# Packed keys: two heads per tile, pair products on array halves, one maximum per pair

## The chip, the cores and the metric

The program runs on one core of one Trainium2 chip. The metric is the device time in microseconds of one execution; the median of three runs is compared. The engines are TensorE (matrix products into PSUM), VectorE, ScalarE, GpSimd (POOL) and SyncE, which issues most of the DMAs. PSUM has eight banks of 512 fp32 columns.

## What is computed

Four layers run over a batch of 4 sequences of 1024 tokens with 256 channels. What matters here is attention, in layers 0, 1 and 3:

```python
s = jnp.einsum('bhqd,bhkd->bhqk', q, k) * scale      # 16 score maps per batch, 16 channels each
s = jnp.where(mask, s, jnp.float32(-jnp.inf))         # causal
p = jax.nn.softmax(s, axis=-1)
out = jnp.einsum('bhqk,bhkd->bhqd', p, v)
```

Layer 0 and layer 3 have 16 heads; layer 1 has 8 differential heads, which are 16 score maps in pairs with a value of 32 channels per pair. Layer 0 goes on with a mixture of experts (2 shared, 16 routed, top 2), layer 1 with a gated FFN, layer 2 has a recurrent mixer and a ternary FFN, layer 3 eight LoRA experts on a gated FFN, top 2.

## The kernel before

Each layer is a loop over the four batches, and each batch a sequence of stages with a barrier between them. A stage is a block in which every engine has its own instruction list, ordered by hand, and engines wait for one another's semaphores. The three layers with attention share four pieces.

`attention_operands` normalises the input, projects q, k and v tile by tile (L354, eight tiles of 128 tokens), rotates q and k on VectorE (L407 to L412), splits each value into an fp16 high part and an fp16 rest (ScalarE L451, L454; POOL L484, L486) and stacks them so that one product over 128 rows gives the full-precision score. A q tile holds two heads of 64 rows each. A k tile holds one head: its 64 rows, and zeros in the other 64, so that k tile times q tile gives one head's score. TensorE turns 8 q and 16 k tiles per token tile (L340, L342) into banks 4 and 5 to 6; VectorE stores q (L369) and ScalarE stores k (L430).

`MaximumPass` finds each query's largest score, so that the exponentials can be shifted. It runs inside the expert stages: TensorE puts a block of scores (L552, up to 512 columns) and, on a diagonal block, a mask product (L555) into a bank, and VectorE reduces the bank to its maximum (L586). 192 blocks and 4 small turns (L545) are dealt out over the slots between the products of the experts by `share_out`. A bank is filled again when VectorE has read it. In layer 0's experts (`experts`: L1154 up, L1139 down, VectorE's sum L1187) the banks are 4 to 7 in turn; in layer 3 (`lora_experts`: L1657, L1660 first products, L1668 second, L1678 lower, L1695 and L1699 down) they are 6 and 7, and bank 6 also serves the low-rank products L1645 and `down`. The low-rank product of the second half of the tokens stands in the middle of the stage. The negated maxima go by DMA (L602) into two rows of each q tile, next to two rows of ones in k.

`attention` works on key tiles: TensorE makes transposed scores of one head (L628) with a mask product on the diagonal block (L631) into one of three pairs of banks (2 to 7), ScalarE takes the exponential (L673), and TensorE multiplies by the values (L647), 17 or 33 output rows for each head side by side in the array, into banks 0 and 1. With maps = 4 (layers 0 and 3) a step is four heads of one key tile: three scores, the values of the step before, the fourth score. With maps = 2 (layer 1) it is two heads: both scores, then the values of two steps before. The width W of a score is 1024 - 128 x (key tile), so a group of eight steps goes from 1024 to 128 columns; there are four groups, or eight in layer 1. L664 stores the sums of a group.

`attention_finish` turns the sums back and divides (L727, L765, L774).

Of the kernel before, what the change touches and what calls it, by code (L numbers as in the profile page):

```python
# [17 lines left out]
P = 128  # L18
# [9 lines left out]
NEG = -1.0e30  # L28
E_SH, E_RT, F0 = 2, 16, 128
# [7 lines left out]
ARENA = 43600  # L37
# [75 lines left out]
def setup_constants(nc, m, io):  # L113

    with stage(nc, "cleared", "selected", "psum_cleared", "tables_in", pool=True) as (block, cleared, selected, psum_cleared, tables_in):
        @block.gpsimd
        def _(pool):
            pool.memset(m.ident[:, :], 0.0).then_inc(cleared, 1)
            pool.memset(m.mask_qk[:, :], 0.0).then_inc(cleared, 1)
            pool.memset(m.mask_kq[:, :], 0.0).then_inc(cleared, 1)  # L120
# [10 lines left out]
            pool.affine_select(out=m.mask_kq[:, :], in_=m.mask_kq[:, :], compare_op=ALU.is_ge, fill=NEG,  # L131
# [165 lines left out]
def attention_operands(nc, m, a, src, batch, out_bias, wqkv, bias, table, rms, heads, vd):  # L297
# [19 lines left out]
    names = ["proj", "taken", "steps", "pool_done", "rotated", "hi", "lo", "stacked", "turned", "stored", "cleared",  # L317
             "rms_in", "rms_std", "squared"]
    with stage(nc, *names, *Normalisation.SEMAPHORES, pool=True) as (block, proj, taken, steps, pool_done, rotated, hi, lo, stacked, turned, stored,
# [3 lines left out]
        def kcols(buf, parity, slot, n=1, step=1):  # L323

            c0 = P * parity + 64 * parity + HD * slot
            v = a.ks[:, buf, :].rearrange("p (n c) -> p n c", c=2 * P)
            if n == 1:
                return v[:, :, c0:c0 + HD]
            return v[:, :, c0:c0 + HD * step * n].rearrange("p n (s c) -> p n s c", c=HD * step)[:, :, :, 0:HD]

        @block.tensor
        def _(pe):
            def turn(t):
                pe.wait_ge(stacked, 3 * (t + 1))
                if t >= 1:
                    pe.wait_ge(stored, 2 * t)
                psq = m.ps[:, 4, :].bitcast(F16)
                psk = m.ps[:, 5:7, :].rearrange("p a b -> p (a b)").bitcast(F16)
                for n in range(NM // 2):
                    pe.transpose(psq[:, n * P:(n + 1) * P], a.qs[:, t % 2, n * P:(n + 1) * P], m.ident_h[:, :])  # L340
                for n in range(NM):
                    last = pe.transpose(psk[:, n * P:(n + 1) * P], a.ks[:, t % 2, n * P:(n + 1) * P], m.ident_h[:, :])  # L342
                last.then_inc(turned, 1)
# [1825 lines left out]
```

## Time and profile before

| | us |
|---|---|
| median of three runs | 5175.5 |
| lowest, highest | 5164.4, 5177.24 |
| span of the profiled execution | 5169.3 |

The span is counted from the first to the last instruction. In a row of the profile `out<-in` names the tensors written and read, the numbers before it are partitions x elements, `x` counts instructions, and a bracket says how long the engine was idle before it and for whose result. An fp32 product shows as two instructions. `PEld` is the load of a product's stationary operand. The end of a product is modelled and lies after the time at which the next may start, so the throughput of TensorE is read from starts.

### The profile page before, as it was taken

Reading aid. Unit: us, or ns where it says so; the run is one execution under the profiler, and the core shown is the slowest. Engines: PE = TensorE matmul, PEld = TensorE weight load, DVE = VectorE, ACT = ScalarE, POOL = GpSimd, SP = SyncE. Lnnn points to the kernel's source line nnn. Section 1 sums busy time; section 2 is a strip of 40 time slices with the busy share of each in tenths; the row PEclk is TensorE's granted clock in tenths of the full one; section 3 lists DMA queues with packets and bytes.
Section 4 is the critical chain, followed back from the end, with each engine's and each line's share of the span. In section 5 each row is a group of like instructions: output and inputs, shape, how many; then the busy total and the mean of one; then the engine's idle time right before and its main releaser. Section 6 shows DMA issues by size and latency. Waiting matters only on the chain. (4 is left out here: it accounts for less than half of the span.)

```text
span 5169.3 us, 62879 instructions
## 1 busy us (share of the span) xinstructions
PE 4168.2 (81%) x22944; PEld 2388.1 (46%) x22944; DVE 2510.8 (49%) x5496; ACT 1934.0 (37%) x3242; POOL 557.6 (11%) x629
## 2 busy tenths in 40 slices
PE   6979979979828979798974786776887898888898
PEld 4635536446313644536352654655344443443443
DVE  5917738459162342415036446446643552651661
ACT  3163261441626355463622323323126116206206
POOL 1001010010011010100000201203211110210220
PEclk9999999989958989899986888888999899999999
DMA  2000000000030000000010000001000000000000
GB/s 81 1 2 1 1 1 1 1 1 1 2 110 1 1 1 1 1 1 1 1 47 0 1 0 0 0 0 43 1 1 9 1 1 10 1 1 10 1 1 9
DMA packets 44814, 45.06 MB, mean 9 GB/s; under 512 B 10320, under 2 KB 40784, under 8 KB 44496
## 3 DMA queue, kind: packets, MB, share of 16 engines
q1 hardware_dynamic: 37424, 31.89, 2.1%
q10 hardware_dynamic: 7072, 9.05, 0.6%
q8 instruction: 184, 3.01, 0.2%
q14 instruction: 134, 1.10, 0.1%
HBM read 36.22 MB, written 4.19 MB: 8 GB/s over the span
## 5 line engine op out<-in xcount | busy, mean ns | idle before, releaser
L586 DVE TENSOR_REDUCE arena<-ps 128x1 f32<-128x512 f32 (+3 forms) x1536 | 779.5, 550 | 219.6 <-PE ps L555 127.7
L673 ACT ACTIVATE arena<-ps 128x1024 f32<-128x1024 f32 (+7 forms) x1024 | 594.1, 660 | 119.5 <-PE ps L631 62.2
L628 PE MATMUL ps<-arena 128*128 128x512 f16 (+3 forms) x1536 | 392.4, 333 | 94.6 <-ACT arena L673 71.0
L552 PE MATMUL ps<-arena 128*128 128x512 f16 (+3 forms) x1536 | 414.6, 328 | 14.2 <-DVE arena L586 12.1
L765 DVE RECIPROCAL small<-ps 128x16 f32<-128x16 f32 x64 | 16.1, 251 | 782.7 <-PE ps L727 782.1
L673 ACT ACTIVATE attention<-ps 128x512 f32<-128x512 f32 (+7 forms) x512 | 302.5, 656 | 116.9 <-PE ps L631 78.1
L631 PE MATMUL ps<-mask_kq,ident_b 128*128 128x128 bf16 x1536 | 323.9, 221 | 0.0
L628 PEld LDWEIGHTS ps<-arena 128*128 128x128 f16 x1536 | 138.5, 98 | 399.3 <-ACT arena L673 336.2
L1732 ACT ACTIVATE arena<-ps 128x512 f32<-128x512 f32 x96 | 53.0, 595 | 681.7 <-PE ps L1668 578.0
L1170 ACT ACTIVATE arena<-ps 128x512 f32<-128x512 f32 x144 | 86.0, 597 | 592.1 <-PE ps L1154 592.0
L1154 PE MATMUL ps<-arena 128*128 128x512 f32 x576 | 302.6, 613 | 0.0
L647 PE MATMUL ps<-arena 128*17 128x512 f32 (+3 forms) x3072 | 297.4, 489 | 2.9 <-ACT arena L673 2.9
L647 PE MATMUL ps<-attention 128*33 128x512 f32 (+3 forms) x1536 | 296.0, 494 | 0.0
L552 PEld LDWEIGHTS ps<-arena 128*128 128x128 f16 x1536 | 144.7, 97 | 314.3 <-DVE arena L586 197.1
L1139 PE MATMUL ps<-arena 128*128 128x256 f32 x1152 | 289.0, 387 | 0.8 <-DVE arena L1187 0.8
L354 PE MATMUL ps<-arena 128*128 128x512 f32 (+1 forms) x768 | 275.3, 508 | 0.0
L782 DVE RECIPROCAL small<-ps 128x16 f32<-128x16 f32 x32 | 8.1, 254 | 496.2 <-PE ps L727 494.9
L1657 PE MATMUL ps<-arena 128*128 128x512 f32 x384 | 207.7, 623 | 27.6 <-DVE arena L1750 18.2
L1139 PEld LDWEIGHTS ps<-arena 128*128 128x128 f32 x1152 | 206.6, 190 | 38.2 <-issue 8.0
L1187 DVE SCALAR_TENSOR_TENSOR arena<-ps,arena 128x256 f32<-128x256 f32 x512 | 217.9, 474 | 10.0 <-PE ps L1139 9.0
L555 PE MATMUL ps<-mask_qk,ident_b 128*128 128x128 bf16 x1024 | 221.2, 220 | 0.0
L628 PE MATMUL ps<-attention 128*128 128x512 f16 (+3 forms) x768 | 202.2, 340 | 15.0 <-PEq L56 14.9
(271 smaller groups left out, 6995.9 us busy)
## 6 DMA issues: line engine op xcount, KB each, us to landing
making<-basis SPq DMA_DIRECT2D x16, 768.0 KB, 4.5
out<-x_all SPq DMA_DIRECT2D x8, 512.0 KB, 3.0
arena<-w_down SPq DMA_DIRECT2D x1, 2304.0 KB, 24.8
x_all<-x SPq DMA_DIRECT2D x2, 1024.0 KB, 13.8
x_all<-x ACTq DMA_DIRECT2D x2, 1024.0 KB, 19.7
arena<-arena SPq DMA_DIRECT2D x128, 4.0 KB
making<-w_gate_up SPq DMA_DIRECT2D x1, 2048.0 KB, 15.2
arena<-w_qkv SPq DMA_DIRECT2D x2, 768.0 KB, 6.2
```

What stands on the lines that cost most here:

```text
L354: last = pe.matmul(m.ps[:, 2 * (t % 2) + j, 0:w], m.xn_t[:, k, t * P:(t + 1) * P], wqkv[:, k, c0:c0 + w], start=(k == 0), stop=(k == KD - 1))
L552: last = pe.matmul(out[:, 0:w], a.q[:, hh // 2, qt * P:(qt + 1) * P], a.k[:, hh, c * CH:c * CH + w], start=True, stop=not diag)
L555: last = pe.matmul(out[:, w - P:w], m.ident_b[:, :], m.mask_qk[:, :], start=False, stop=True)
L586: dve.reduce_max(a.mp[:, h, qt, c:c + 1], out[:, 0:w], AX.X).then_inc(self.block_out, 1)
L628: last = pe.matmul(m.ps[:, bank + c, q0 - c * CH:CH], a.k[:, h, kt * P:(kt + 1) * P], a.q[:, h // 2, q0:(c + 1) * CH], start=True, stop=no ...
L631: last = pe.matmul(m.ps[:, bank + c, q0 - c * CH:q0 - c * CH + P], m.ident_b[:, :], m.mask_kq[:, :], start=False, stop=True)
L647: last = pe.matmul(m.ps[width * hh:width * hh + w, c, q0 - c * CH:CH], a.v[:, kt, vh, :], p, start=(kt == 0), stop=(kt == TC * (c + 1) - 1))
L673: act.activation(a.p[:, u % ring, kt * P:S], m.ps[:, bank:bank + 2, :].rearrange("p a b -> p (a b)")[:, kt * P:S], ACT.Exp, scale=HD ** -0 ...
L1139: last = pe.matmul(product(n, j), f.mid[:, n % 3, j * P:(j + 1) * P], wdown[:, e, :], start=True, stop=True)
L1154: last = pe.matmul(m.ps[:, n % 2, :], wup[:, e, k, :], m.xn_t[:, k, c * CH:(c + 1) * CH], start=(k == 0), stop=(k == KD - 1))
L1187: dve.scalar_tensor_tensor(m.acc[:, t, :], out, f.gate_w[:, t, e - E_SH:e - E_SH + 1], m.acc[:, t, :], ALU.mult, ALU.add).then_inc(added, 1)
L1657: pe.matmul(m.ps[:, 2 * (n % 2) + j, :], wt[:, k, i * P:(i + 1) * P], m.xn_t[:, k, c * CH:(c + 1) * CH], start=(k == 0), stop=False)
```

## The change

Keys are packed as queries are: a k tile holds two heads of 64 rows. A score product names the 64 rows of its head, so the two heads of a pair work on the two halves of the array and into different banks. The parts:

- `attention_operands`: 16 transposes per token tile instead of 24, into two alternating pairs of banks; one ScalarE instruction stores q and k; VectorE's store is gone; ScalarE and POOL write k in one instruction each instead of two.
- `MaximumPass`: an item is a block of two heads: two mask products first (on a diagonal block), then the two halves' products, then one maximum over 2 x w values. 96 items and 4 turns. In `experts` the items take the bank pairs 4, 5 and 6, 7 in turn; in `lora_experts` they all take 6, 7.
- `attention`: no mask product; a step scores its pairs, then does values. For key tiles 4 to 7 the two heads of a pair share one pair of banks and one exponential. VectorE cuts what lies above the diagonal by a minimum with a triangle of 3e38 and 0, in place, and values wait for that.
- `lora_experts`: both low-rank products at the start, in banks 4, 5 and 2, 3; `down` in banks 4, 5 and 0, 1; the order around the middle is other.

```diff
             def turn(t):
-                pe.wait_ge(stacked, 3 * (t + 1))
-                if t >= 1:
-                    pe.wait_ge(stored, 2 * t)
...
+                pe.wait_ge(stacked, 2 * (t + 1))
+                if t >= 2:
+                    pe.wait_ge(stored, t - 1)
...
-            def store(t):
-
-                dve.wait_ge(turned, t + 1)
-                dve.tensor_copy(a.q[:, :, t * P:(t + 1) * P],
-                                m.ps[:, 4, :].bitcast(F16).rearrange("p (n c) -> p n c", c=P)).then_inc(stored, 1)
...
+                act.activation(a.qk_t[:, :, :, t * P:(t + 1) * P].rearrange("p n j c -> p j n c"),
+                               m.ps[:, b0:b0 + 2, :].bitcast(F16).rearrange("p j (n c) -> p j n c", c=P),
+                               ACT.Copy).then_inc(stored, 1)
...
-        last = pe.matmul(out[:, 0:w], a.q[:, hh // 2, qt * P:(qt + 1) * P], a.k[:, hh, c * CH:c * CH + w],
-                         start=True, stop=not diag)
+        pair = g * self.maps // 2 + j
         if diag:
-            last = pe.matmul(out[:, w - P:w], m.ident_b[:, :], m.mask_qk[:, :], start=False, stop=True)
-        last.then_inc(self.block_in, 1)
+            for odd in range(2):
+                pe.matmul(out[:, odd, w - P:w], m.ident_b[:, :], m.mask_qk[:, :], start=True, stop=False,
+                          skip_group_check=True)
+        for odd in range(2):
+            half = slice(64 * odd, 64 * odd + 64)
+            last = pe.matmul(out[:, odd, 0:w], a.q[half, pair, qt * P:(qt + 1) * P],
+                             a.k[half, pair, c * CH:c * CH + w], start=not diag, stop=True, skip_group_check=True)
+        last.then_inc(self.pair_in, 1)
...
-        dve.reduce_max(a.mp[:, h, qt, c:c + 1], out[:, 0:w], AX.X).then_inc(self.block_out, 1)
+        dve.reduce_max(a.mp[:, 2 * j:2 * j + 2, qt, c], out[:, :, 0:w], AX.X).then_inc(self.pair_out, 1)
...
+                s = first_slot[v]
+                end = first_slot[v + 1]
+                if end > 3:
+                    pe.wait_ge(exped, end - 3)
...
+                    for odd in range(2):
+                        half = slice(64 * odd, 64 * odd + 64)
+                        b = bank(s + odd) + c if kt < TC else bank(s) + odd
+                        last = pe.matmul(m.ps[:, b, q0 - c * CH:CH], a.k[half, pair, kt * P:(kt + 1) * P],
+                                         a.q[half, pair, q0:(c + 1) * CH], start=True, stop=True)
...
-                pe.wait_ge(exped, maps * (n + 1))
+                pe.wait_ge(masked, pairs * (n + 1))
...
-                for hh in range(maps):
-                    score(maps * n + hh)
-                    if hh == maps // 2 and n >= lag:
-                        values(n - lag)
+                for j in range(pairs):
+                    score(pairs * n + j)
+                if n >= lag:
+                    values(n - lag)
...
+                dve.wait_ge(exped, first_slot[v + 1])
+                diag = a.p[:, 2 * v % ring:2 * v % ring + 2, kt * P:(kt + 1) * P]
+                dve.tensor_tensor(diag, diag, keep, ALU.min).then_inc(masked, 1)
...
-        mp.share_out([((n, i), up if i < KD else (per_step - KD * up) / TC, (4, 5, 6, 7))
+        mp.share_out([((n, i), up if i < KD else (per_step - KD * up) / TC, (4, 6))
...
-        fixed = {"down": 1, "second": 1.5, "lower": 0}
+        fixed = {"down": 0.5, "second": 0.5}
...
-        mp.share_out([(key, fixed.get(key[0], rate), (7,) if key[0] == "down" else (6, 7)) for key in slots])
+        mp.share_out([(key, fixed.get(key[0], rate), (6,)) for key in slots])
...
             pe.wait_ge(*weights)
             low(0)
+            low(1)
```

## Rows read from the trace of the kernel before

**Rows 1.** The page's first part: busy time of each engine.
```profile
PE 4168.2 (81%) x22944; PEld 2388.1 (46%) x22944; DVE 2510.8 (49%) x5496; ACT 1934.0 (37%) x3242; POOL 557.6 (11%) x629
```

**Rows 2.** Stretches: length, then busy PE, PEld, DVE, ACT, POOL, clock, DMA.
```profile
91.90:266.50 174.60, 171.12 (x786) 106.66 (x785) 159.97 (x399) 24.37 (x39) 0.00 (x0) 0.99 0.00 1
268.40:362.60 94.20, 83.25 (x704) 30.15 (x704) 0.00 (x0) 78.65 (x137) 0.00 (x0) 1.00 0.00 1
378.60:432.50 53.90, 37.13 (x272) 25.92 (x272) 40.49 (x82) 32.20 (x43) 15.46 (x24) 0.90 0.01 2
1601.30:1719.70 118.40, 117.66 (x704) 39.32 (x704) 0.00 (x0) 83.83 (x145) 0.00 (x0) 0.99 0.00 1
3637.00:3838.80 201.80, 184.54 (x712) 88.97 (x712) 131.18 (x252) 13.24 (x24) 45.65 (x36) 0.99 0.00 1
```

**Rows 3.** Timeline of layer 0's operands: start, length, engine, line.
```profile
46.25 0.68 DVE L381 TENSOR_TENSOR arena<-ps,arena 128x512 f32<-128x512 f32 x1
...
49.99 0.68 DVE L381 TENSOR_TENSOR arena<-ps,arena 128x512 f32<-128x512 f32 x1
...
62.59 0.68 DVE L369 COPY arena<-ps 128x1024 f16<-128x1024 f16 x1
...
63.19 0.68 DVE L381 TENSOR_TENSOR arena<-ps,arena 128x512 f32<-128x512 f32 x1
...
64.96 1.88 ACT L430 ACTIVATE arena<-ps 128x2048 f16<-128x2048 f16 x1 [1.01 <-PE ps L342]
...
67.03 0.68 DVE L369 COPY arena<-ps 128x1024 f16<-128x1024 f16 x1
```

**Rows 4.** Timeline of the same stage, the last turn.
```profile
80.27 0.61 PE L340 MATMUL ps<-ident_h,arena 128*128 128x128 f16 x8 [2.06 <-ACT arena L430]
```

**Rows 5.** Timeline of TensorE in layer 0's attention.
```profile
292.07 0.38 PE L628 MATMUL ps<-arena 128*128 128x512 f16 x1
...
292.29 0.22 PE L631 MATMUL ps<-mask_kq,ident_b 128*128 128x128 bf16 x1
...
293.32 0.38 PE L628 MATMUL ps<-arena 128*128 128x512 f16 x1
...
293.63 0.41 PE L647 MATMUL ps<-arena 128*17 128x128 f32 x8
...
297.12 1.91 PE L647 MATMUL ps<-arena 128*17 128x512 f32 x16
...
298.97 0.34 PE L628 MATMUL ps<-arena 128*128 128x384 f16 x1
```

**Rows 6.** Groups of L586 by form, whole span: busy, mean ns, idle before.
```profile
L586 DVE TENSOR_REDUCE arena<-ps 128x1 f32<-128x512 f32 x768 | 513.2, 684 | 132.9 <-PE ps L552 83.2 <-PE ps L555 44.3
...
L586 DVE TENSOR_REDUCE arena<-ps 128x1 f32<-128x128 f32 x256 | 72.1, 282 | 13.1 <-PE ps L555 11.4
```

**Rows 7.** Layer 0's attention: timeline, and the group of the widest exponentials.
```profile
292.76 3.77 ACT L673 ACTIVATE arena<-ps 128x1024 f32<-128x1024 f32 x4 [0.21 <-PE ps L628]
...
293.97 0.39 PE L628 MATMUL ps<-arena 128*128 128x512 f16 x1
...
303.29 2.60 ACT L673 ACTIVATE arena<-ps 128x768 f32<-128x768 f32 x4 [0.65 <-PE ps L628]
...
315.74 3.77 ACT L673 ACTIVATE arena<-ps 128x1024 f32<-128x1024 f32 x4 [0.21 <-PE ps L628]
...
L673 ACT ACTIVATE arena<-ps 128x1024 f32<-128x1024 f32 x16 | 15.1, 1028 | 0.6 <-PE ps L628 0.6
```

**Rows 8.** Line L774: an operation of VectorE over 256 values, min/median/max ns.
```profile
L774 DVE TENSOR_TENSOR x_all<-arena x32: 424/425/426, 365.0 to 1418.1; 128x256 f32 x32
```

**Rows 9.** Timeline of TensorE in the LoRA stage: idle time at the seam and in `down`.
```profile
3715.63 1.98 PE L1645 MATMUL ps<-arena 128*128 128x512 f32 x4 [1.57 <-DVE arena L1748]
...
3719.93 1.10 PE L1657 MATMUL ps<-arena 128*128 128x512 f32 x2 [2.32 <-DVE arena L1750]
...
3820.73 1.10 PE L1695 MATMUL ps<-arena 128*128 128x256 f32 x4 [2.15 <-issue]
```

More of the change, by code:

```diff
@@ L316, in attention_operands, with slots @@
         cos, sin = ([v.rearrange("p (h c) -> p h c", c=HD)] * NT for v in table)
-    names = ["proj", "taken", "steps", "pool_done", "rotated", "hi", "lo", "stacked", "turned", "stored", "cleared",
+    names = ["proj", "taken", "steps", "pool_done", "rotated", "hi", "stacked", "turned", "stored", "cleared",
              "rms_in", "rms_std", "squared"]
-    with stage(nc, *names, *Normalisation.SEMAPHORES, pool=True) as (block, proj, taken, steps, pool_done, rotated, hi, lo, stacked, turned, stored,
+    with stage(nc, *names, *Normalisation.SEMAPHORES, pool=True) as (block, proj, taken, steps, pool_done, rotated, hi, stacked, turned, stored,
                                cleared, rms_in, rms_std, squared, *norm_sems):
         norm = Normalisation(m, src, a.xn, m.xn_t, norm_sems, xload=batch, bias=out_bias)
[L323 to L329, printed above, removed]
+        def slots(stack, buf):
+            return stack[:, buf, :].rearrange("p (h s c) -> p h s c", h=NM, c=HD)
         @block.tensor
@@ L506, in __init__ @@
             i = 0
-            for h in range(self.maps):
+            for j in range(self.maps // 2):
                 for qt in range(NT):
                     for c in range(qt // TC + 1):
-                        self.items.append(("block", g, h, qt, c))
+                        self.items.append(("pair", g, j, qt, c))
                         i += 1
@@ L527, in share_out, with pair_banks @@
         assert len(self.banks) == len(self.items)
-    def bank(self, n):
-        return self.m.ps[:, self.banks[n], :]
+    def pair_banks(self, n):
+        return self.m.ps[:, self.banks[n]:self.banks[n] + 2, :]
     def tensor_item(self, pe, n):
         m, a = self.m, self.a
-        out = self.bank(n)
+        out = self.pair_banks(n)
         if self.items[n][0] == "turn":
@@ L608, in attention @@
 def attention(nc, m, a, maps, width):
-    groups = NM // maps
-    n_exp = NM * NT
+    groups, pairs = NM // maps, maps // 2
+    n_pair = pairs * groups * NT
     ring = a.p.shape[1]
     lag = 1 if maps == 4 else 2
-    with stage(nc, "scored", "exped", "summed", "evac") as (block, scored, exped, summed, evac):
+    first_slot, slots = [], []
+    for v in range(n_pair):
+        first_slot.append(len(slots))
+        if v // pairs % NT < TC:
+            slots += [(v, 0), (v, 1)]
+        else:
+            slots += [(v, None)]
@@ L616, in _, with place, bank, score @@
+    first_slot.append(len(slots))
+    def place(v):
+        n, j = divmod(v, pairs)
+        g, kt = divmod(n, NT)
+        return g, kt, g * pairs + j
+    def bank(s):
+        return 2 + 2 * (s % 3)
+    with stage(nc, "scored", "exped", "masked", "summed", "evac") as (block, scored, exped, masked, summed, evac):
         @block.tensor
         def _(pe):
-            def score(u):
-                n, hh = divmod(u, maps)
-                g, kt = divmod(n, NT)
-                h = g * maps + hh
-                if u >= 3:
-                    pe.wait_ge(exped, u - 2)
-                bank = 2 + 2 * (u % 3)
+            def score(v):
+                g, kt, pair = place(v)
+                s = first_slot[v]
+                end = first_slot[v + 1]
+                if end > 3:
+                    pe.wait_ge(exped, end - 3)
@@ L681, in _ @@
             store(groups - 1, 1)
+        @block.vector
+        def _(dve):
+            keep = m.tri[:, :].unsqueeze(1).broadcast_to([P, 2, P])
+            for v in range(n_pair):
+                g, kt, pair = place(v)
+                dve.wait_ge(exped, first_slot[v + 1])
+                diag = a.p[:, 2 * v % ring:2 * v % ring + 2, kt * P:(kt + 1) * P]
+                dve.tensor_tensor(diag, diag, keep, ALU.min).then_inc(masked, 1)
 def attention_finish(nc, m, a, maps, width, wout, out_scale, batch=None, stored=None):
```

222 lines of the change are left out of this document (97 added, 125 removed).

## Prediction, made before the changed kernel was run

> **What bounds the kernel now.** I read the page's first part, then one stretch per stage, then the instructions inside each. TensorE is busy 81% of the 5169.3 us span [rows 1], an average over unlike stages. One batch of each, in [rows 2]: the experts stage has TensorE at 171.1 of 174.6 us, VectorE at 160.0 beside it, so TensorE bounds it. Layer 0's attention has TensorE 83.3 and ScalarE 78.7 of 94.2: neither alone, but the chain between them. Layer 1's attention has TensorE 117.7 of 118.4. Layer 0's operands (53.9) have nothing full over the stage; inside it VectorE runs without gaps. The LoRA stage has TensorE 184.5 of 201.8, and 131.2 of VectorE. Each occurs four times, except that layer 3's attention and operands are like layer 0's: eight of those.
>
> **Operands (saves).** VectorE starts a period at 62.59 with the q store L369 and the next at 67.03: 4.43 us without a gap, of which L369 takes 0.60 (62.59 to 63.19). A period without it, 46.25 to 49.99, is 3.74 [rows 3]. The store goes to ScalarE, which already spends 1.88 on 2048 values of k; q and k together are again 2048. ScalarE's copies go from 0.63 + 2 x 0.40 to about 2 x 0.63, the POOL differences from three to two of the same size, the transposes from 24 to 16 per tile. None reaches 3.7 us a period (ScalarE 1.88 + 1.26; TensorE 2.6 of projections + 0.9). Five stores lie ahead of the last rotation: 5 x 0.6 = 3.0. At the end the last turn waited 2.06 for ScalarE's previous store [rows 4]; with two PSUM pairs it waits for POOL alone, 1.9 less. Together about 5.0 a stage (bounds 3 and 6.5), layer 1 the same: 12 x 5.0 = -60 us.
>
> **What a pair costs TensorE.** A full-array fp16 product of 512 columns holds it 0.215 us (292.07 to the mask at 292.29), or 0.42 ns a column, so a mask of 128 takes 0.055. The product at 293.32 has streamed by 293.53, but the narrow values product starts at 293.63. The 16 narrow ones from 297.12 go in four groups of four, 0.435 a group, so they have streamed by 298.87; the full product starts at 298.97. A change of array form costs 0.10 each way [rows 5]. No row shows the array split by rows. Split by columns the four products of a group run at once: 16 of 0.43 us take 1.91 and not 7 [rows 5]. I take row halves as equally concurrent, the nearest row (bound above: one after the other, as full products go), and the switch as 0.095 each way (bounds 0 and 0.19, two loads of 0.10 behind each drain).
>
> The Trainium skill, TensorEngine Tiling (Array Packing), Key Properties, says a change of tiling mode drains TensorE, without a price; by it alone splitting costs something wherever other forms stand between, and the row above prices it.
>
> **Experts (about nothing).** 192 blocks hold 16 heads x 4608 causal columns = 30.7 us of products; concurrent pairs save half, 15.4. Masks stay 128. Laying the 100 items on the slots by the code gives 91 runs of pair products between full-array work: 91 x 0.19 = 17.3. VectorE's maximum falls a little: 512 columns take 0.684, 128 take 0.282 [rows 6], so 1.05 ns a column plus 0.15; two joined save a start-up of 0.07 to 0.15, 96 times, hidden beside TensorE. But it now frees a pair only after 1.22 us and there are two pair buffers; I add 2 us. Sum +4 a stage (bounds -12 and +20), 4 x = +16.
>
> **Attention of layers 0 and 3 (saves).** Four exponentials of 1024 take 3.77, one 1.03: 0.91 apart (0.904 by the starts), which is W/1.2 + 51 ns; of 768, 0.69. But before the fourth of each step ScalarE sits idle, 0.65 at 768 [rows 7]; per group of eight steps the starts at 292.76 and 315.74 are 22.98 apart against 17.95 of work. The cause: the fourth score stands behind the values product. At W = 768 the chain is release 0.31 (an exponential lasts 0.12 beyond its slot, 1.03 against 0.904, and the product after it starts 0.19 later), score 0.32 + 0.06, switch, values of 896 at 1.67 ns = 1.49, switch, score up to its last product 0.16, and 0.38 to completion: 2.9, against three exponentials 2.07; stall 0.8, measured 0.65 to 0.8. The new order (both pairs, then values) gives: exponential 0.69, release 0.31, pair 0.32, switch 0.1, values 1.49, switch 0.1, next pair to its last product 0.05, completion 0.42, less 0.1 by which this sum exceeded the trace above: 3.38 a step against 2.76 of ScalarE work. In the same way W = 896 gives 3.8 and 640 3.0; W = 1024, behind short values, has ScalarE alone, 4 x 0.904 and a store of 512 columns at the same rate, 0.48: 4.15. The four joined steps need 6.6: ScalarE 5.2, plus the wait that the change adds. Values now wait for VectorE's minimum (256 values: 0.42 [rows 8] and two hand-overs, about 0.55), behind which TensorE's next scores queue; at the widths 256 and 128 two slots of exponentials (0.96, 0.53) don't cover it. Group 21.0, four 84, start-up 2.3: 86.5 against 94.2, -7.5 (bounds -14, ScalarE alone, and -3), 8 x = -60 us. The 128 masks leave, and ScalarE has 32 start-ups of 51 ns fewer; both are inside this sum.
>
> **Layer 1's attention (saves).** Per step TensorE does W/2.4 x 2 + 0.11 + 0.19 of scores, masks, switches and W/600 of values two steps back. Taking the larger of that and ScalarE's step, a group is 1.81 + 1.60 + 2.65 + 2.33 + 2.0 + 1.69 + 1.36 + 1.05 + a store 0.48 = 15.0; eight give 120 for 118.4, so the reading holds. With concurrent pairs and no masks: 1.81 + 1.60 + 2.2 + 1.95 + 1.68 + 1.42 + 1.15 + 0.88 + 0.48, plus 0.25 since a pair waits for the first half of the one before: 13.4, eight 107: -11.5 (bounds -18, -4), 4 x = -46 us.
>
> **LoRA stage (costs).** Before, the maxima had banks 6 and 7: TensorE filled one while VectorE read the other. Now all items use the one pair 6, 7, and each of the six slots of a unit has 1.15 items and only one fp32 product (0.86) between. From one item to the next for 512 columns: two masks 0.11, switch 0.095, product to completion 0.38, hand-over 0.04, maximum of 1024 values 1.22 (from 0.684 and 0.282 [rows 6]), hand-over 0.06: 1.90. TensorE's own work in that time: 0.11 + 0.19 + 0.21 + 0.86 = 1.37. Stall 0.53; at 384 columns 0.26, at 256 and 128 none; over the mix of twelve (6, 2, 2, 2) 0.31. An item directly behind another stalls 1.1. Per unit five of the first and one of the second, 2.6; 12 units 31 us. Behind TensorE's wait queue the next FFN products, and VectorE's gates behind those. Switches 92 x 0.19 = 17.5 against 15.4 saved. In return the second low-rank block moves from the middle to the front, where six VectorE operations (4.3) hold up the first items, TensorE some 3.5. The waits of the seam go: by starts 1.1, 1.7, 2.5 and 1.0, the second and third shown as 1.57 and 2.32 of idle; of `down` 1.1 twice, 1.2 and 2.3 (2.15 shown), two others of 1.6 and 0.9 [rows 9]: 14.5 in all. Waits of the old items, 3.9, go. Sum 31 + 2 + 3.5 - 14.5 - 3.9 + 2 for late gates = +20 (bounds 0 and +32), 4 x = +80 us.
>
> **Sum.** -60 + 16 - 60 - 46 + 80 = -70. Against the profiled 5169.3: 5099; the median of the runs is 6.2 above it, so 5105.
>
> **Rivals.** A: the halves run one behind the other. Place: every pair. Price: 15.4 in each of eight maximum passes = 123; in attention the pair lies on the chain, 7.6 x 8 = 61 and 6.1 x 4 = 24; together +208, 5313. It decides once the second product starts a third of the first's streaming (about 72 ns of 215) behind it. For: no row shows a row split. Against: the column split [rows 5]. Halfway, if each run of pairs loads its two weights behind the drain (0.095 more, 183 runs x 4): +70, 5175. The Trainium skill, TensorE: Matmul & The Clock Gate, Measured speedup vs the span model, has four row tiles at 3.07 times. By an estimate from that figure a pair would take 0.65 of serial, not 0.5, and the time would be 5167; it belongs to the halfway case.
>
> B: the single pair buffer of the LoRA stage costs nothing, since the stage has slack elsewhere: -80, 5025. For: 17 of its 201.8 us are idle time of TensorE now [rows 2]. Against: TensorE is in order, and each item must wait for a read of 1.22. C: the change leaves ScalarE and TensorE of attention coupled as before, another order but the same stalls; then -60 and -46 shrink to -20 and -25: 5166. For: the minimum adds a link; against: the fourth score no longer stands behind values.
>
> **How the numbers follow.** Forecast 0.66 (own range 5060 to 5150), A in full 0.12, halfway 0.08, B 0.07, C 0.07. Predicted 5105. Range 5030 to 5195: it leaves out A and the far half of B. A measurement of this kernel tells 0.3%, 15.5 us, from no change: below 5160 are nearly all of the forecast (0.64), B and a little of halfway and C, 0.74; within, parts of both, 0.09; above, A and the rest, 0.17.
>
> **What would show it.** Row-half products starting within 20 ns of each other; a gap of about 0.1 around each run; operands near 49, layer 1's 5 shorter too; layer 0's attention near 87, layer 1's near 107; experts within 5 of 174.6; LoRA near 222, with TensorE waiting for L586's successor. I am wrong if the second half starts late (experts above 190), or if the LoRA stage is not longer.

## The result and the profile after

The changed kernel takes 5199.8 us (median of four runs, 5198.2 to 5202.95) against 5175.3 for the kernel before (four runs too, 5164.4 to 5177.2). The ratio is 1.0053, with a 95% interval from 1.0039 to 1.0067. So it is slower, by a little more than the 0.3% that can be told from no change. The prediction was 5105, with 5030 to 5195 as its range: the sign was wrong, and the time lies outside the range.

The profiled execution of the changed kernel has a span of 5197.9 us, 28.6 more than before. Its first part answers to [rows 1]:

```profile
PE 3998.3 (77%) x20640; PEld 2097.8 (40%) x20640; DVE 2748.2 (53%) x5400; ACT 1889.1 (36%) x2762; POOL 511.6 (10%) x521
```

Every engine but VectorE does less: TensorE 170 us less, ScalarE 45 less. The time went up all the same. These are the stretches that answer to [rows 2]: experts, layer 0's attention, the LoRA stage, layer 1's attention and layer 0's operands. The columns are the length, busy PE, PEld, DVE, ACT and POOL, the granted clock of TensorE, and DMA.

```profile
88.10:269.20 181.10, 176.30 (x784) 97.62 (x783) 156.89 (x303) 24.38 (x39) 0.00 (x0) 0.99 0.00 1
271.00:365.00 94.00, 66.61 (x574) 13.95 (x572) 26.87 (x64) 75.33 (x105) 0.00 (x0) 0.85 0.00 1
3586.00:3817.00 231.00, 201.61 (x720) 83.49 (x718) 128.97 (x162) 13.87 (x25) 45.12 (x36) 0.97 0.00 1
1610.80:1720.10 109.30, 96.08 (x576) 23.14 (x572) 27.21 (x64) 81.49 (x113) 0.00 (x0) 0.96 0.00 1
378.30:430.80 52.50, 35.11 (x208) 23.57 (x208) 36.01 (x74) 30.77 (x35) 14.23 (x20) 0.79 0.01 2
```

The second row is the one to stop at. The stage has 17 us less of TensorE and 3 less of ScalarE than in [rows 2], and it is as long as before (94.3 us for 94.1 by first and last instruction; the other seven take 94.1 to 97.4). The number that changed for the worse is the granted clock, 0.85 instead of 1.00. The sums over the whole program, each stage counted from its start to the start of the next, are as follows. The products of the router, the first 7 us of an experts stage, are counted with the operands ahead of it.

| stages | before | forecast | measured change |
|---|---|---|---|
| operands, 12 | 780.7 | -60 | -62.3 |
| experts, 4 | 704.8 | +16 | +26.3 |
| attention, layers 0 and 3, 8 | 759.4 | -60 | +12.3 |
| attention, layer 1, 4 | 478.5 | -46 | -38.8 |
| LoRA experts, 4 | 844.9 | +80 | +85.9 |
| all others | | 0 | +5.2 |

Of the 98.6 us that the forecast is off, 72.3 lie in one line. Of the 5.2 at the foot, 4.3 are layer 3's pair routing, at a granted clock of 0.54 to 0.55 where it was 0.57 to 0.61.

Now the clock within one group of eight steps, layer 0, first batch. The four stretches are cut where the granted clock changes (same columns):

```profile
281.91:298.98 17.07, 11.78 (x122) 2.75 (x120) 5.54 (x14) 14.87 (x22) 0.00 (x0) 1.00 0.01 2
298.98:305.80 6.82, 5.23 (x24) 0.75 (x24) 1.17 (x3) 4.04 (x6) 0.00 (x0) 0.50 0.00 0
305.80:322.87 17.07, 11.59 (x120) 2.75 (x120) 5.87 (x14) 15.09 (x23) 0.00 (x0) 1.00 0.00 1
322.87:326.28 3.41, 2.76 (x16) 0.62 (x20) 0.47 (x2) 3.13 (x4) 0.00 (x0) 0.50 0.02 5
```

The clock is at 1.00 (2.4 GHz), falls to 0.50 (1.2 GHz) for 3.4 to 13.7 us, and comes back; this happens once in every group of every such stage. In the kernel before it was 1.00 over the whole stretch of this stage [rows 2]; four of its eight stages have one fall of 3.4 us in their first microseconds, and none falls later. TensorE's timeline around the fall:

```profile
294.43 0.61 PE L635 MATMUL ps<-arena 64*128 64x512 f16 x4
296.15 0.61 PE L635 MATMUL ps<-arena 64*128 64x512 f16 x4 [1.11 <-ACT arena L681]
296.69 0.41 PE L652 MATMUL ps<-arena 128*17 128x128 f32 x8
297.98 0.55 PE L635 MATMUL ps<-arena 64*128 64x384 f16 x4 [0.88 <-ACT arena L681]
300.20 0.93 PE L635 MATMUL ps<-arena 64*128 64x384 f16 x4 [1.66 <-ACT arena L681]
301.06 3.61 PE L652 MATMUL ps<-arena 128*17 128x512 f32 x16
304.60 0.82 PE L635 MATMUL ps<-arena 64*128 64x256 f16 x4
```

In the widest steps ScalarE sets the pace, the paired products are done in half the time, and TensorE stands still for 1.11, 0.88 and 1.66 us. Then come the widest values, L652, and they run at half speed: 3.61 us, where the same sixteen took 1.91 [rows 5]. ScalarE waits for what is queued behind them:

```profile
295.07 3.77 ACT L681 ACTIVATE arena<-ps 128x1024 f32<-128x1024 f32 x4 [0.51 <-PE ps L635]
...
299.18 1.77 ACT L681 ACTIVATE arena<-ps 128x896 f32<-128x896 f32 x2
301.16 1.73 ACT L681 ACTIVATE arena<-ps 128x896 f32<-128x896 f32 x2 [0.21 <-PE ps L635]
305.45 2.92 ACT L681 ACTIVATE arena<-ps 128x768 f32<-128x768 f32 x4 [2.57 <-PE ps L635]
308.86 2.54 ACT L681 ACTIVATE arena<-ps 128x640 f32<-128x640 f32 x4 [0.48 <-PE ps L635]
...
318.40 2.85 ACT L681 ACTIVATE arena<-ps 128x1024 f32<-128x1024 f32 x3 [0.51 <-PE ps L635]
```

A group is 318.40 - 295.07 = 23.33 us, against 22.98 before [rows 7] and a forecast of 21.0. One wait of 2.57 us holds most of what is missing.

The changed kernel's own stages bear this out, since they have the same instructions and differ in how long the clock is low. Those with 27.3 us at 1.2 GHz take 94.1 to 94.3 us, the one with 30.7 takes 96.1, and those with 34.0 to 34.1 take 96.6 to 97.4.

### The profile page after: what moved, and what is told of

It reads as the page before. It is cut to its first block and busy times, and to the rows that moved or that the text cites. A ratio compares the mean times of both kernels' runs of the same rounds, so it can differ in the third digit from the quotient of the medians.

```text
span 5197.9 us, 56899 instructions
## 1 busy us (share of the span) xinstructions
PE 3998.3 (77%) x20640; PEld 2097.8 (40%) x20640; DVE 2748.2 (53%) x5400; ACT 1889.1 (36%) x2762; POOL 511.6 (10%) x521
## 5 line engine op out<-in xcount | busy, mean ns | idle before, releaser
L572 DVE TENSOR_REDUCE arena<-ps 128x2 f32<-128x1024 f32 (+3 forms) x768 | 725.5, 956 | 329.1 <-PE ps L540 326.9
L698 DVE TENSOR_TENSOR arena<-arena,tri 128x256 f32<-128x256 f32 x512 | 214.9, 425 | 553.1 <-ACT arena L681 449.3
L681 ACT ACTIVATE arena<-ps 128x768 f32<-128x768 f32 (+3 forms) x512 | 408.0, 868 | 116.5 <-PE ps L635 115.6
L652 PE MATMUL ps<-arena 128*17 128x512 f32 (+3 forms) x3072 | 352.0, 566 | 42.3 <-DVE arena L698 42.3
L635 PE MATMUL ps<-arena 64*128 64x512 f16 (+3 forms) x1536 | 220.3, 369 | 191.1 <-ACT arena L681 170.5
L652 PE MATMUL ps<-attention 128*33 128x512 f32 (+3 forms) x1536 | 302.7, 503 | 0.0
L698 DVE TENSOR_TENSOR attention<-attention,tri 128x256 f32<-128x256 f32 x256 | 108.8, 425 | 354.2 <-ACT attention L681 238.9
L540 PE MATMUL ps<-arena 64*128 64x512 f16 (+3 forms) x1536 | 258.4, 337 | 18.3 <-DVE arena L572 18.0
L536 PEld LDWEIGHTS ps<-mask_qk,ident_b 128*128 128x128 bf16 x1024 | 81.1, 98 | 354.3 <-DVE arena L572 225.8
L681 ACT ACTIVATE attention<-ps 128x1024 f32<-128x1024 f32 (+3 forms) x256 | 205.5, 876 | 38.9 <-PE ps L635 35.0
L900 PE MATMUL ps<-ffn_parts,weight_parts 128*128 128x512 f32 x768 | 188.2, 407 | 13.9 <-DVE ffn_parts L982 13.9
L536 PE MATMUL ps<-mask_qk,ident_b 128*128 128x128 bf16 x1024 | 144.7, 223 | 67.6 <-DVE arena L572 67.0
L1825 POOL TENSOR_TENSOR arena<-arena 128x512 f32<-128x512 f32 x96 | 121.4, 1265 | 721.0 <-DVE arena L1765 721.0
```

The costliest lines, as they stand in the source:

```text
L536: pe.matmul(out[:, odd, w - P:w], m.ident_b[:, :], m.mask_qk[:, :], start=True, stop=False, skip_group_check=True)
L540: last = pe.matmul(out[:, odd, 0:w], a.q[half, pair, qt * P:(qt + 1) * P], a.k[half, pair, c * CH:c * CH + w], start=not diag, stop=True, ...
L572: dve.reduce_max(a.mp[:, 2 * j:2 * j + 2, qt, c], out[:, :, 0:w], AX.X).then_inc(self.pair_out, 1)
L635: last = pe.matmul(m.ps[:, b, q0 - c * CH:CH], a.k[half, pair, kt * P:(kt + 1) * P], a.q[half, pair, q0:(c + 1) * CH], start=True, stop=True)
L652: last = pe.matmul(m.ps[width * hh:width * hh + w, c, q0 - c * CH:CH], a.v[:, kt, vh, :], p, start=(kt == 0), stop=(kt == TC * (c + 1) - 1))
L681: act.activation(a.p[:, u + odd, kt * P:S], m.ps[:, b:b + 2, :].rearrange("p a b -> p (a b)")[:, kt * P:S], ACT.Exp, scale=HD ** -0.5).the ...
```

## The experiments

Theory T: attention of layers 0 and 3 is as predicted, but with less to do TensorE stands still longer in the widest steps, its granted clock falls once a group, and the values behind run at half speed. Rivals: R1, the wait for VectorE's minimum costs more than I gave it; R2, the wait of a pair for two slots at once does.

**Needless products on top of the changed kernel.** If T holds, more work makes the kernel faster.

```diff
+                if maps == 4 and kt < 2 and v > 0 and v % (pairs * NT) > 0:
+                    if g >= 1:
+                        pe.wait_ge(evac, NC * (g - 1) + 1)
+                    for _ in range(3):
+                        pe.matmul(m.ps[:, 0, :], a.k[:, pair, 0:P], a.q[:, pair, 0:CH], start=True, stop=True)
                 if end > 3:
                     pe.wait_ge(exped, end - 3)
```

> The changed kernel with three needless full-array products of 512 columns (0.215 us each at 2.4 GHz) ahead of three pairs of scores in each group of layers 0 and 3's attention, the second pair of key tile 0 and both of key tile 1, where TensorE waited 0.88 to 1.66 us for ScalarE; they go into bank 0 before that group's values. Theory T (attention of layers 0 and 3 did not get shorter because TensorE's granted clock fell to 0.5 once in every group, behind these idle stretches): the clock stays at 1.0 inside the stage, a group falls from 23.3 us to near 21, the stage from 94 to 97 down to 86 to 89, the whole from 5200 to about 5140. Rival R1 (the wait for VectorE's minimum is the cause) and R2 (a pair waits for two slots at once): the added products can only cost, whole 5200 to 5215, stage 94 or more whatever the clock does.

Measured: 5128.7 us, ratio to the kernel before 0.992 (0.9904 to 0.9937). The eight stages take 85.9 to 87.3 us (here and below the length of a stage goes from its first instruction to its last). Stretches of this kernel in place of those shown above, and its ScalarE timeline:

```profile
281.00:298.00 17.00, 13.85 (x129) 3.39 (x129) 5.86 (x14) 15.02 (x23) 0.00 (x0) 1.00 0.01 2
298.00:305.00 7.00, 5.33 (x48) 1.19 (x48) 1.70 (x4) 6.03 (x9) 0.00 (x0) 1.00 0.01 2
```

```profile
293.40 3.77 ACT L686 ACTIVATE arena<-ps 128x1024 f32<-128x1024 f32 x4 [0.51 <-PE ps L640]
297.03 0.63 ACT L674 ACTIVATE arena<-ps 128x512 f32<-128x512 f32 x1
297.50 3.40 ACT L686 ACTIVATE arena<-ps 128x896 f32<-128x896 f32 x4
301.38 2.92 ACT L686 ACTIVATE arena<-ps 128x768 f32<-128x768 f32 x4 [0.48 <-PE ps L640]
304.79 2.54 ACT L686 ACTIVATE arena<-ps 128x640 f32<-128x640 f32 x4 [0.49 <-PE ps L640]
307.77 1.94 ACT L683 ACTIVATE arena<-ps 128x1024 f32<-128x1024 f32 x2 [0.45 <-PE ps L640]
...
314.33 3.77 ACT L686 ACTIVATE arena<-ps 128x1024 f32<-128x1024 f32 x4 [0.51 <-PE ps L640]
```

The clock stays at 1.00 once the first microseconds of a stage are over (a fall of 3.1 to 6.8 us is left there), the wait of 2.57 is 0.48, and the group is 314.33 - 293.40 = 20.93 us. The eight stages took 759.4 before, 771.7 after the change and 698.5 with the useless products: the 61 us that the prediction promised were there, behind the clock. R1 and R2 fall as the main cause. The Trainium skill, TensorE: Matmul & The Clock Gate, A second HAM failure mode: psum-queue depth-cycling, tells of a kernel in which short, frequent idle stretches between groups of products made the clock go up and down; the rows here agree with that.

**Fewer, or smaller, needless products.** `range(3)` becomes `range(1)`:

> As the kernel with three needless products in three places of each group of layers 0 and 3's attention, but with one product (0.215 us) in each place: TensorE's idle stretches of 0.88 to 1.66 us stay mostly open. T: the clock still falls in some groups; stages between 86 and 94, whole between 5130 and 5190, the time going with the number of falls in the trace. If the gain of the three products had come from anything but the clock (the order of waits, say), one would give it in full: all stages at 86 to 87, whole near 5130, whatever the clock.

Measured: one run of 5153.1, layer 0's stages 88.6 each, layer 3's 89.5 to 89.8. The falls in the middle of the stage are gone but for one at 71 to 72 us in each of layer 3's; the one at the start lasts 10.2 us instead of 3.4 to 6.8. A part of the products gives a part of the gain, and not the whole of it, as it would if the clock had no part in it.

With three products again, but over 64 rows of the array (`a.k[0:64, pair, 0:P], a.q[0:64, pair, 0:CH]`):

> As the kernel with three needless products in three places, but each of them over 64 rows only: the same 0.215 us each and 512 columns, half of the array at work. T1, what counts for the granted clock is the time TensorE streams: clock 1.0 and stages of 86 to 87 as with full products, whole near 5130. T2, what counts is how much of the array works: half the effect, so falls of the clock remain in some groups, stages 88 to 94, whole 5145 to 5190.

Measured: one run of 5146.5, stages 87.9 to 89.7, one fall left in the middle of five of the eight. This fits T2, the same streaming time over half of the rows holding the clock up less, but it rests on one run, 18 us above that with full products. The full products are also of another form than the pairs beside them, and that wasn't held apart from the number of rows.

These runs and the changed kernel give the price of the clock. Over the eight stages the time at 1.2 GHz and the sum of the stages are 242.1 and 771.7 us in the changed kernel, 95.1 and 720.7 with one product in each place, 84.5 and 716.7 with three over 64 rows, 33.5 and 698.5 with three over 128. From each of these to the last it is 0.35 or 0.36 us of time for every us at the low clock, whatever the products were.

**The same products in the kernel before, as a control.**

```diff
+                if maps == 4 and (kt, hh) in ((0, 2), (1, 0), (1, 2)):
...
+                    for _ in range(3):
+                        pe.matmul(m.ps[:, 0, :], a.k[:, h, 0:P], a.q[:, h // 2, 0:CH], start=True, stop=True)
```

> Control: the kernel before with the same three needless products of 512 columns in the same three places of a group. Its clock is at 1.0 all through the stage without them, so theory T expects no gain: stages of layers 0 and 3 from 94.1 to 97, whole 5170 to 5195. A gain of more than 1 us a stage would mean that the products help by something other than the clock.

Measured: one run of 5187.5, stages 96.3 to 97.5. Near what was expected: they cost 2 to 3 us a stage where the clock needs no help.

**No minimum of VectorE in attention.** The block of VectorE goes, so that nothing above the diagonal is cut, and

```diff
-                pe.wait_ge(masked, pairs * (n + 1))
+                pe.wait_ge(exped, first_slot[pairs * (n + 1)])
```

> The changed kernel without VectorE's minimum in attention: values wait for the exponentials alone, so the part of a diagonal tile above the diagonal is not cut. R1: a hand-over and 0.42 us leave the chain in most steps, a group is 1 to 2 us shorter, the stage of layers 0 and 3 goes from 94 to 97 to near 88, the whole to about 5145. T: the clock falls as before in every group; only the narrow steps gain (two waits of 0.5 to 0.6 us a group), stage 92 to 95, whole 5175 to 5190. R2: the same as T.

Measured: 5168.5, ratio 0.9996 (0.9987 to 1.0006). The stages take 91.4 to 94.0, and the clock falls in every group as before. So R1 holds for a part, 742.2 instead of 771.7 over the eight stages, but not for the miss. A part of those 29.5 is clock in turn, since the time at 1.2 GHz is 211.0 us instead of 242.1. To read the price of the minimum without the clock in it, the same with the three needless products:

> The changed kernel with the needless products and without VectorE's minimum in attention (values wait for the exponentials alone, the diagonal tiles are not cut). At a clock of 1.0 this gives the price of the minimum in the chain. The prediction had it covered in the wide steps and let it cost 0.5 us in each of two or three narrow steps of a group: stage 86.0 to between 81 and 84. If it is wholly covered: 86; if it is on the chain in every step: 0.5 x 32 = 16 us less, 70 to 75.

Measured: one run of 5112.1, stages 83.5 to 84.9, in sum 677.7 against 698.5 with the minimum. The minimum costs 2.6 us a stage, 0.65 a group, inside the 2 to 5 us a stage that I had expected. That is about one uncovered wait in a group.

**The causal cut back on TensorE.** The minimum goes, and ahead of each pair of scores on the diagonal:

```diff
+                    if diag:
+                        for b in place_of:
+                            pe.matmul(m.ps[:, b, q0 - c * CH:q0 - c * CH + P], m.ident_b[:, :], m.mask_kq[:, :],
+                                      start=True, stop=False, skip_group_check=True)
```

> The changed kernel with the causal cut of attention put back on TensorE: 128 mask products a stage of 128 columns (0.055 us each, 7 us a stage) ahead of the pair's scores, and no minimum of VectorE. T: with 7 us more of products the granted clock falls less or not at all; if not at all, stage 88 to 90 and whole near 5145; if it falls as before, stage about 96 and whole 5200 or more. R1: the link is gone, stage 88 to 91 with the same falls of the clock.

Measured: 5311.1, ratio 1.0276 (1.0259 to 1.0293), worse than all I had expected. Layers 0 and 3 take 101.9 to 103.5 with the clock falling still. The price is read in layer 1, where TensorE sets the time: 489.3 instead of 439.8, 12.4 us a stage, 0.19 for each of its 64 pairs. Two masks are 0.11; the rest, 0.08, is near one more change of form, since full-array masks now stand between narrow values and the pair. That it is this change of form was argued from the size and not tested. A mask that cost 0.055 among full-array products costs 0.1 there.

**One part of the change alone: the masks taken out of the kernel before.**

> The kernel before without the 128 mask products of 128 columns in each attention stage (the diagonal tiles are not cut), all else as it was. T: taking only TensorE's work away (7 of 83 us a stage in layers 0 and 3) brings the clock down to 0.5 now and then, which it never was, so the stage is no shorter than 94.2 or longer; in layer 1, where TensorE sets the time, it is shorter by up to 7. R1 and R2 (the clock is not the cause): layers 0 and 3 at clock 1.0 and 2 to 4 us shorter, as each fourth score comes 0.055 to 0.11 us sooner; whole about 5125.

Measured: 5129.6, ratio 0.9922 (0.9905 to 0.9938), near the 5125 of the other case. The clock part of T said that falls would begin; apart from one of 3 us in the first 8 us of four stages, much as in the kernel before, they did not:

```profile
269.40:360.20 90.80, 76.56 (x576) 21.94 (x576) 0.00 (x0) 78.55 (x137) 0.00 (x0) 1.00 0.00 1
```

The stage is 3.3 us shorter at a clock of 1.00, and layer 1's are 5.5 shorter. The 7 us of masks alone aren't what held the clock up.

**One part alone: the order.** In the kernel before, `if hh == maps // 2` becomes `if hh == maps - 1`, so that the values come after all four scores.

> One part of the change alone: the kernel before with all four scores of a step ahead of the values of the step before (masks and full-array products as before). By the chain of the prediction a step of W = 768 is 0.69 + 0.31 + 0.38 + 0.1 + 1.49 + 0.1 + 0.54 = 3.6 us, as before, so without a fall of the clock the stage stays at 93 to 96 and the whole within 20 of 5170. If the order is what makes the clock fall (the idle stretches ahead of the last score are as long as in the changed kernel), falls to 0.5 show in it once a group and the stage is 97 or more; if the halved streaming of the pairs is needed for it, the clock stays at 1.0.

Measured: one run of 5173.1, stages 94.6 to 94.8, and no fall but a short one in the first microseconds. The order alone neither gains anything nor brings the falls. A stretch of one whole group and a little more:

```profile
294.00:318.00 24.00, 21.51 (x187) 7.69 (x179) 0.00 (x0) 19.81 (x36) 0.00 (x0) 1.00 0.00 1
```

**The order undone in the changed kernel**, with the values between the two pairs:

> One part of the change undone: the changed kernel with the values of the step before placed between the two pairs of scores again (in layer 1, where a step is one pair, nothing changes). The second pair then stands behind values that wait for the last minimum; at W = 768 that is 0.55 + 0.1 + 1.49 + 0.1 + 0.4 against 1.38 us of exponentials of the first pair, a stall of some 1.2 us a step, step 4.0 instead of 3.4. If the order alone was worth what the prediction gave it: stages of layers 0 and 3 at 100 to 108, whole 5240 to 5310. If TensorE's idle stretches decide and not the halving of its work, the clock now falls at other places or not at all, and the stage comes to under 97.

Measured: one run of 5446.0, stages 123.3 to 126.3. This is far above my 100 to 108. The stage has TensorE busy for 78.77 of 124.80 us at a clock of 0.77, and the clock falls twice a group. The stall and the clock weren't held apart. Layer 0's first stage spends 58.5 of 124.9 us at 1.2 GHz; by an estimate, if all of that took half the time, 95.6 would be left, which is still 9 more than the forecast for the new order. By that estimate pairs need the new order, and how much the clock adds was again left out of my figure.

**Which part brings the falls?** Neither the order nor the missing masks did it alone. That left the pairs themselves, by their halved streaming time or by their form, or parts together. In the kernel before, layers 0 and 3, with the order changed and no masks:

```diff
-                    diag = c == kt // TC
+                    diag = c == kt // TC and maps == 2
+                    if maps == 4:
+                        q0 += ((c + 1) * CH - q0) // 2
```

> The kernel before, with full-array score products, in layers 0 and 3 with the last half of each product's columns only, no mask products, and the values after all four scores; ScalarE reads all columns as ever, with scale 0 since half of them are old (scores, cut and exponentials are left out in effect, the instructions stay). TensorE streams scores for 15.4 us a stage, as the pairs of the changed kernel do side by side, but in the form of the kernel before. H1, the halved streaming time brings the falls of the clock: falls to 0.5 once a group, stage 89 to 96. H2, the row-split form or its switches bring them: clock 1.0 through the stage, 84 to 88 us.

Measured: one run of 5151.1, stages 89.8 to 94.7, and falls to 0.5 in the middle of all eight, at about 28, 51 and 75 us of the stage where there are three, as in the changed kernel. Its stretches around the first, and TensorE's values in it:

```profile
281.00:297.73 16.73, 11.22 (x112) 4.01 (x112) 0.00 (x0) 14.60 (x29) 0.00 (x0) 1.00 0.01 1
297.73:301.15 3.42, 3.42 (x16) 0.42 (x15) 0.00 (x0) 1.99 (x3) 0.00 (x0) 0.50 0.00 0
301.15:318.00 16.85, 12.49 (x126) 4.48 (x122) 0.00 (x0) 14.55 (x29) 0.00 (x0) 1.00 0.00 1
```

```profile
297.34 0.37 PE L630 MATMUL ps<-arena 128*128 128x192 f16 x2 [0.93 <-ACT arena L675]
297.64 3.58 PE L649 MATMUL ps<-arena 128*17 128x512 f32 x16
```

These are full-array products; no row is split. So H2 is out: the falls come without the row-split form. They come with halved streaming, the new order and no masks together. That the halving is needed isn't shown, since order and missing masks together with full columns weren't run, nor the halves alone with the old masks kept among them.

**The LoRA stage: how much is the single pair of banks?** VectorE's maximum there reads `out[:, :, 0:w // 2]`.

> The changed kernel with VectorE's maximum in the LoRA stage reading only the first half of each block's columns (the rest is left out of the maximum), so a pair of banks comes free about 0.5 us sooner for w = 512. Theory U (the single pair of banks is the largest part of what the LoRA stage lost): the stage falls by the stalls of the sum, 20 to 30 us, from 231 to between 201 and 211, whole 5085 to 5120. Rival V (the loss is form switches and the start of the stage): the stage falls by under 8 us, whole over 5165. The other stages stay as after the change.

Measured: 5113.1 (two runs), ratio 0.9891 (0.9871 to 0.9911). The stage takes 206.4 to 206.6 instead of 231.1, 24.6 less. What TensorE's loads waited for, in one LoRA stage of the changed kernel and then of this one (total, times, longest):

```profile
PEld ps L536 <- DVE arena L572: 50.8, 50, 2.6
PEld ps L540 <- DVE arena L572: 21.1, 23, 1.6
```

```profile
PEld ps L536 <- DVE arena L572: 29.8, 48, 2.4
PEld ps L540 <- DVE arena L572: 17.6, 23, 1.1
```

The two kinds of wait together fall from 71.9 to 47.4 us, and U holds. A part of the 24.6 is clock: the changed kernel spends 13.7 us of that stage at 1.2 GHz, this one 3.4, which can be worth up to 5 us. A ring of two there needs a pair of banks that the stage doesn't have; it wasn't tried. The attention of layers 0 and 3 has the same code in both and was expected to stay, yet it took 781.3 us in sum against 771.7, with 262.6 us at 1.2 GHz against 242.1: how long each fall lasts isn't fixed by the stage's own instructions.

**A version that beats both.** Needless products in attention, and no mask products in the maximum pass:

```diff
-        if diag:
-            for odd in range(2):
-                pe.matmul(out[:, odd, w - P:w], m.ident_b[:, :], m.mask_qk[:, :], start=True, stop=False,
-                          skip_group_check=True)
```

> A candidate that should beat both kernels: the changed kernel with the three needless products in attention, and the maximum taken over whole diagonal blocks, without the 128 mask products in each maximum pass (a maximum over more keys is still a bound that every exponential is shifted by; the causal cut itself stays in attention). The masks go from TensorE's path: 128 x 0.055 = 7 us in each of eight stages, and in the LoRA stage also from the chain from one block to the next. Expected: experts 181 to 174, LoRA 231 to 222, whole 5129 to about 5065. If the masks were hidden by VectorE's maxima or by other waits: under 2 us a stage, whole above 5112.

Measured: 5061.8, ratio 0.9792 (0.9776 to 0.9809). Experts 173.5 to 175.2 (7.1 less on average than with the needless products alone, 128 x 0.055 = 7.0), LoRA 219.1 to 221.8 (10.0 less), attention 86.3 to 87.5. The kernel before has the same mask products in its maximum pass; what leaving them out would save there wasn't run.

**Separate waits for the two halves of a pair**, on top of that, key tiles 0 to 3:

> The candidate with needless products and without masks in the maxima (5062), and in attention each half of a pair of key tiles 0 to 3 waits for its own slot, the even head's products ahead of the odd head's. R2 (the wait for two slots at once costs): the first half's exponential can start 0.3 to 0.9 us sooner in the wide steps, stage from 86 to 82 to 84, whole near 5035. Against: in the wide steps ScalarE was already nearly gapless, and at 768 and 640 the products of a pair no longer run side by side (0.2 us more): stage 86 to 88, whole 5060 to 5075.

Measured: 5055.7, ratio 0.9769 (0.975 to 0.9788), against 5061.8 for the version without it; these were timed on different occasions, so the 6 us are not certain. Five of the eight stages are 85.6 with no fall of the clock at all, the others 87.1 to 87.4:

```profile
602.80:688.40 85.60, 73.48 (x612) 18.57 (x612) 26.84 (x64) 75.03 (x105) 0.00 (x0) 1.00 0.01 1
```

R2 was worth under 1 us a stage in these traces, not the 2 to 4 that it claimed. ScalarE has 75.0 of these 85.6 us, so little is left.

## Why the prediction was wrong, point by point

**Attention of layers 0 and 3: the step that failed.** "The new order gives ... 3.38 a step", "group 21.0 ... 86.5 against 94.2". The chain itself was right to 0.1 us a step once the clock held (its own terms for W = 1024 add up to 4.10, not to the 4.15 that it gives):

| step | forecast | needless products kernel | from |
|---|---|---|---|
| W = 1024 | 4.15 | 4.10 | 297.50 - 293.40 |
| 896 | 3.8 | 3.88 | 301.38 - 297.50 |
| 768 | 3.38 | 3.41 | 304.79 - 301.38 |
| 640 | 3.0 | 2.98 | 307.77 - 304.79 |
| four joined | 6.6 | 6.56 | 314.33 - 307.77 |

What failed is the duration of the values in that chain. The step took it (1.49 for 896 columns, 1.91 for 1024) from a stage with TensorE busy for 83 of 94 us at a clock of 1.00 [rows 2, 5], and put it into a stage with 67 of 94, where the widest ones took 3.61, a group 23.33 instead of 21.0, and the eight stages 12.3 us more instead of 60 less. I read the granted clock in [rows 2] as a fact of the chip and not as something that the kernel before earned by being busy. In these stages, where ScalarE sets the pace of the wide steps, the saving on TensorE was paid for by the products that remain. None of the rivals was this. C comes near in time (5166), but by a stall of order that isn't there, and my bound of -3 a stage excluded any loss.

**Operands: right.** -62.3 for -60. VectorE's period is 3.87 us (64.83 - 60.96), where [rows 3] have 4.43 with the q store and 3.74 without:

```profile
60.96 0.68 DVE L371 TENSOR_TENSOR arena<-ps,arena 128x512 f32<-128x512 f32 x1
...
64.83 0.68 DVE L371 TENSOR_TENSOR arena<-ps,arena 128x512 f32<-128x512 f32 x1
```

**What a pair costs: right.** The two halves run side by side, and a change of form costs 0.10. LoRA stage of the changed kernel:

```profile
3653.49 0.39 PE L540 MATMUL ps<-arena 64*128 64x512 f16 x2
...
3653.82 1.12 PE L1669 MATMUL ps<-arena 128*128 128x512 f32 x2
```

Two products of 512 columns take 0.39, as long as one of [rows 5] (0.38), and the next product starts 0.33 after them: 0.215 of streaming and 0.11 for the change. Rival A is dead, in full and halfway. The Trainium skill, TensorEngine Tiling (Array Packing), Key Properties, states that drain without a price; the row gives it one.

**Experts: +26 for +16**, 6.5 a stage and not 4, inside the bounds. The sum of masks is exact (7.1 for 7.0 in the version without them); which of the others, the switches or the two pairs of banks, holds the 2.5 us was not taken apart.

**Layer 1's attention: -39 for -46.** Stages 108.3 to 109.3 for a forecast of 107. TensorE sets the time here and stays busy (the clock is 0.96 over the stage). One low stretch lies at the start, where the operands before it had a clock of 0.76 to 0.80. It lasts 7.6 to 9.8 us, against 3.2 to 5.0 in the kernel before, and within the changed kernel the stages with 2.1 us more of it take 1.1 us longer. By that, an estimate, it cost some 2 us a stage, which is about what the forecast missed (-9.7 for -11.5). The prediction had the clock at nothing here too.

**LoRA: +86 for +80**, close in its parts, but in part by luck. VectorE's maximum of 1024 values takes 1.23 (forecast 1.22), and from one item of 512 columns to the mask of the next, at once behind it, are 3663.68 - 3661.74 = 1.94 (forecast 1.90):

```profile
3661.74 0.28 PE L536 MATMUL ps<-mask_qk,ident_b 128*128 128x128 bf16 x2 [0.27 <-DVE arena L572]
...
3662.39 1.23 DVE L572 TENSOR_REDUCE arena<-ps 128x2 f32<-128x1024 f32 x1 [0.71 <-PE ps L540]
3663.68 0.28 PE L536 MATMUL ps<-mask_qk,ident_b 128*128 128x128 bf16 x2 [1.33 <-DVE arena L572]
```

The stalls of 31 us a stage that the prediction gave to the single pair of banks stand beside 24.6 won by reading half. Rival B is dead. The sum had no term for the clock, yet the stage has 13.7 us at 1.2 GHz where the kernel before had 3.4. In the runs with needless products one LoRA stage had 6.8 of it and took 228.4 us instead of 231.1; by that, an estimate, the clock is some 4 of the 21.5 us that the stage grew, so the other terms together were 2 to 3 us a stage too high.

**The range.** Its terms were bounded by rows, and each but one lay within its bounds. The one that didn't, -3 to -14 a stage with +1.5 on average measured, had bounds from the same chain as its value. Bounds that share the assumption of the value don't bound it.

## What to carry to other kernels

Before a saving on TensorE is booked, ask whether TensorE sets the time in that stage. Where it doesn't, durations taken from the trace before hold only as long as the granted clock does: name the products that would run at half speed and price them twice, here 1.7 us for the widest values and 2.4 us a group. After a change, compare the clock of each stage before anything else; a few products that do nothing, put where TensorE waits anyhow, test for it in one run and can be the cure. And a mask of another form placed next to split products can cost a change of form as well: here 0.1 instead of 0.055 us.

## What the runs showed of the hardware that I had not expected

- The granted clock fell from 2.4 to 1.2 GHz where TensorE stood still for 1.7 us at most around the fall, and was busy for 11.78 of the 17.07 us before it; with 13.85 busy of 17.00 it stayed. In the kernel with halved columns it also stayed behind 12.49 of 16.85 (rows above). These are single stretches and give no limit.
- Adding 36 products, 7.7 us of them, to each of eight stages made the program 71 us faster (5199.8 to 5128.7).
- With needless products over 64 rows the eight stages had 84.5 us at 1.2 GHz and the program took 5146.5 us (a single run); with the same columns over 128 rows they had 33.5, and it took 5128.7.
- Each us at 1.2 GHz in these stages cost 0.35 us of time.
- Row halves of the array run fully side by side: two products in 0.39 us.
